# A two-layer graph network on one core: layer 0's edge bias moves from TensorE's bias products to VectorE's additions on the gathered rows

## The reference, cut to what matters

```python
e = edge_attr @ W_edge + b_edge
msg = relu(x[src] + e)
agg = segment_sum(msg, dst, num_segments=x.shape[0])
h = (1.0 + eps) * x + agg
h = relu(h @ W1 + b1) @ W2 + b2      # then batch norm, relu, residual, layer norm
```

## Time and profile before

| | us |
|---|---|
| median of 3 runs | 5301.25 (5294.39 to 5304.22) |
| the profiled execution's own time | 5306.98 |
| its span, first to last instruction | 5305.1 |
| layer 0's edge loop in it | from about 30 to about 2535 |
| layer 1's edge loop in it | from about 2617 to the end |

### The profile page before, as it was taken

One profiled execution on the slowest core, in us unless ns is written; L12 is line 12 of the kernel. 1 busy time (PEld: TensorE's weight loads), 2 busy tenths in 40 slices (PEclk: granted clock), 3 DMA queues, 4 the chain that ended last, 5 costly groups with the idle time before them and its releaser, 6 DMA issues.

```text
span 5305.1 us, 63952 instructions
## 1 busy us (share of the span) xinstructions
PE 3940.2 (74%) x19180; PEld 2743.8 (52%) x19281; DVE 2240.2 (42%) x4481; ACT 718.8 (14%) x1302; POOL 3028.8 (57%) x3229
## 2 busy tenths in 40 slices
PE   6777777778877777777677777776776777777776
PEld 4555555556655555555544444444444444444444
DVE  4333333233332332323544445544555455555555
ACT  2121111112221221112400000000000001001001
POOL 6666656566655555555455555555655555555553
PEclk9888888888888888888877877887877887877777
DMA  4444444344443443433544444444443444443432
GB/s 147 130 132 132 129 126 130 119 131 133 125 129 118 131 128 115 123 115 101 143 122 117 121 120 123 125 120 119 125 119 116 120 124 125 120 123 111 118 114 81
DMA packets 321270, 650.08 MB, mean 123 GB/s; under 512 B 149823, under 2 KB 170537, under 8 KB 321225
## 3 DMA queue, kind: packets, MB, share of 16 engines
q0 software_dynamic: 150272, 413.00, 27.0%
q1 hardware_dynamic: 164681, 230.37, 13.9%
q10 hardware_dynamic: 6272, 6.19, 0.4%
HBM read 636.22 MB, written 13.08 MB: 122 GB/s over the span
## 4 chain that ended last, share of the span: by engine, by line
PE 39%; another core or an unknown queue 24%; issue 18%; DVEq 9%; DVE 8%; ACT 1%; DMA 0%; ACTq 0%; SPq 0%; POOLq 0%
PE psum L685 14%; PE psum L998 7%; PE psum L687 7%; PE psum L1009 5%; DVEq L1152 3%; DVE rows L1136 2%; PE psum L995 1%; DVEq L821 1%; DVE hot_t L854 1%; DVE rows L933 1%; DVEq L863 1%; PE psum L1037 1%; DVEq L1147 1%; DVEq L859 1%
## 5 line engine op out<-in xcount | busy, mean ns | idle before, releaser
L407 POOL DMA_INDIRECT rows<-z_tab,idx x1568 | 1500.3, 957 | 1150.0 <-issue 452.7
L407 POOL DMA_INDIRECT rows<-in_x,idx x1568 | 1491.4, 951 | 1012.4 <-issue 454.2
L685 PE MATMUL psum<-onehot,rows 128*128 128x128 f32 x6272 | 1345.2, 340 | 379.6 <-issue 374.8
L685 PEld LDWEIGHTS psum<-onehot,rows 128*128 128x128 f32 x6272 | 992.9, 223 | 792.1 <-issue 787.5
L1136 DVE TENSOR_TENSOR rows<-rows,psum 128x1024 f32<-128x1024 f32 x392 | 475.6, 1221 | 1706.1 <-remote 1065.9
L998 PE MATMUL psum<-weights,edge_room 128*128 128x256 f32 x3136 | 899.5, 411 | 120.5 <-issue 84.7
L1009 PE MATMUL psum<-rows,onehot 128*128 128x256 f32 x3136 | 860.1, 411 | 130.6 <-issue 126.0
L687 PE MATMUL psum<-onehot,rows 128*4 128x128 f32 x3136 | 687.2, 303 | 129.3 <-issue 128.5
L998 PEld LDWEIGHTS psum<-weights,edge_room 128*128 128x128 f32 x3136 | 658.0, 210 | 233.5 <-issue 78.8
L1009 PEld LDWEIGHTS psum<-rows,onehot 128*128 128x128 f32 x3136 | 627.9, 207 | 263.4 <-issue 184.5
L1082 ACT ACTIVATE rows<-rows 128x1024 f32<-128x1024 f32 x392 | 414.3, 1057 | 1981.3 <-DVE rows L1136 1565.6
(11 more groups left out here) (152 smaller groups left out, 1461.5 us busy)
## 6 DMA issues: line engine op xcount, KB each, us to landing
dst_t<-in_dst_jp SPq DMA_DIRECT2D x197, 512.0 KB
edge_room<-in_edge_t SPq DMA_DIRECT2D x196, 512.0 KB
rows<-in_x,idx POOLq DMA_INDIRECT x1568
rows<-z_tab,idx POOLq DMA_INDIRECT x1568
z_tab<-edge_room SPq DMA_DIRECT2D x14, 455.0 KB, 6.5
idx<-in_src_idx SPq DMA_DIRECT2D x392, 4.0 KB
dst_t<-in_x_t SPq DMA_DIRECT2D x14, 448.0 KB
rows<-in_x_t SPq DMA_DIRECT2D x14, 448.0 KB, 5.1
```

Source lines behind the costliest of these rows:

```text
L407: nc.gpsimd.indirect_dma_start(rows[0:count, u, j, 0:width], None, table, bass.IndirectOffsetOnAxis(ap=idx[0:count, u, j:j + 1], axis=0)). ...
L685: pe.matmul(banks[first + k][:, 0:WIN], rows[:, u, j, k * P:(k + 1) * P], hot, start=(j == 0), stop=(j == J - 1))
```

## The change

The bias products and everything that prepares them go. DVE adds `b_edge`, broadcast over four edges, to each half of the gathered rows, in two instructions ahead of the group's first `add_edges`, with a drain behind them. The edge products now start their banks themselves.

```diff
--- before.py
+++ after.py
@@ -156,10 +156,6 @@
         is_before = early[:, 32 * D:32 * D + GROUPS]
         wz_tmp = early[:, 40 * D:44 * D].rearrange("p (m n) -> p m n", n=D)
         att = hot_t[:, :].bitcast(F32).rearrange("p (a n) -> p a n", a=2)
-        bias_rest = early[:, 36 * D:38 * D].rearrange("p (a n) -> p a n", a=2)
-        bias_part = early[:, 38 * D:39 * D].bitcast(BF16).rearrange("p (a n) -> p a n", a=2)
-        bias_rhs = onehot[:, 2, 0:2, :].rearrange("p j n -> p (j n)").bitcast(BF16)
-        ones_bf = onehot[:, 2, 2, 0:P // 2].bitcast(BF16)
         plan_f = early[0:1, 24 * D:24 * D + 3 * GROUPS].rearrange("p (a n) -> p a n", a=3)
 
 
@@ -260,7 +256,7 @@
                 self.dst_in = [s(f"dst_in_{u}_") for u in range(2)] if n else []
 
         layer0, layer1 = Layer(0), Layer(1)
-        half_done, added, bias_ready = sem("half_done"), sem("added"), sem("bias_ready")
+        half_done, added = sem("half_done"), sem("added")
         a_sum = sem("a_sum")
 
         def two(name):
@@ -990,13 +986,9 @@
                     pe.wait_ge(layer0.edge_in[u], 16 * i + 16)
                 if not (first_round(i) and g == 0):
                     pe.wait_ge(added, 2 * g + b - 1)
-                for q in range(2):
-                    bank = banks[2 * b + q]
-                    pe.matmul(bank[:, 0:2 * D], ones_bf[:, :], bias_rhs[:, :], start=True, stop=False)
-                    for h in range(2):
-                        j = 4 * b + 2 * q + h
-                        last = pe.matmul(bank[:, h * D:(h + 1) * D], edge_in[:, u, j * P:(j + 1) * P], w_edge[:, :],
-                                         start=False, stop=(h == 1))
+                for j in range(4 * b, 4 * b + 4):
+                    last = pe.matmul(banks[j // 2][:, (j % 2) * D:(j % 2 + 1) * D], edge_in[:, u, j * P:(j + 1) * P],
+                                     w_edge[:, :], start=True, stop=True)
                 return last
 
             def sum_half(u, g, b, early):
@@ -1060,7 +1052,6 @@
                 pe.wait_ge(a_act2, c + 1)
                 second_product(c)
 
-            pe.wait_ge(bias_ready, 1)
             pe.wait_ge(const_in, 16 * WEIGHT_LOADS)
             c0 = rounds(pe, body, finish_nodes)
             u = lambda g: g % RING
@@ -1130,6 +1121,10 @@
             def step():
                 dve.drain()
 
+            def add_bias(u, b):
+                half = rows[:, u, 4 * b:4 * b + 4, 0:D]
+                dve.tensor_tensor(half, half, b_edge[:, :].unsqueeze(1).to_broadcast([P, 4, D]), ALU.add)
+
             def add_edges(i, u, g, b):
                 dve.wait_ge(half_done, 2 * g + b + 1)
                 half = rows[:, u, 4 * b:4 * b + 4, 0:D]
@@ -1153,6 +1148,9 @@
 
             def body(i, u, g):
                 dve.wait_ge(layer0.rows_in[u], 16 * J * (i + 1))
+                add_bias(u, 0)
+                add_bias(u, 1)
+                dve.drain()
                 add_edges(i, u, g, 0)
                 make_onehot(u, g)
                 if not (first_round(i) and g < 3):
@@ -1516,25 +1514,6 @@
             dve.drain().then_inc(wz_cols, 1)
 
             dve.wait_ge(edge_w_in, 48)
-            dve.memset(ones_bf[:, :], 1.0)
-            dve.tensor_copy(bias_part[:, 0, :], b_edge[:, :])
-            step()
-            dve.tensor_tensor(bias_rest[:, 0, :], b_edge[:, :], bias_part[:, 0, :], ALU.subtract)
-            step()
-            dve.tensor_copy(bias_part[:, 1, :], bias_rest[:, 0, :])
-            step()
-            dve.tensor_tensor(bias_rest[:, 1, :], bias_rest[:, 0, :], bias_part[:, 1, :], ALU.subtract)
-            dve.tensor_scalar(bias_rhs[:, 0:D], bias_part[:, 0, :], ident[:, 0:1], None, ALU.mult)
-            step()
-            dve.tensor_copy(bias_rhs[:, D:2 * D], bias_rest[:, 1, :])
-            dve.scalar_tensor_tensor(bias_rhs[:, 0:D], bias_part[:, 1, :], ident[:, 1:2], bias_rhs[:, 0:D],
-                                     ALU.mult, ALU.add)
-            step()
-            dve.scalar_tensor_tensor(bias_rhs[:, 0:D], bias_rhs[:, D:2 * D], ident[:, 2:3], bias_rhs[:, 0:D],
-                                     ALU.mult, ALU.add)
-            step()
-            dve.tensor_copy(bias_rhs[:, D:2 * D], bias_rhs[:, 0:D])
-            dve.drain().then_inc(bias_ready, 1)
 
             dve.wait_ge(dst_in, 48)
             dve.tensor_copy(first_f[:, :], firsts[:, 0, :])
```

## The result

The change makes the kernel faster. It was measured twice more, on two chips: 0.9929 (0.9899 to 0.9959) and 0.9899 (0.9876 to 0.9922). The prediction had 5382 us, a loss of 1.5%.

The account below looks back on a forecast made before the run. Layer 0 was taken as bound by POOL: runs of gathers, each with a tail of 2 to 4 us. -13 - 2 + 96 = +81 us on the profiled 5306.98 gave 5388, or 5382 against the runs shown; range 5290 to 5480.

Parts of the forecast that it names:

- Gathers held: POOL's gathers in layer 0, held when starting under DVE's SBUF additions: 0.5 us a group, +96 us, bounds 0 and +419.
- Absorbed: Rival, POOL's waits in layer 0: the holds come off the 2.9 us of waits, 5305 down to 5290; chance 0.12.
- Bias products off PE: Restarts after layer 0's 14 chunk ends: fewer products before the edge product, -13 us, bounds 0 and -24; start -2.
- DVE: Two additions and drain per layer 0 group: 2.6 us, 510 us in all, hidden in DVE's idle time, so zero.
- DVE late: Rival, behind long waits: additions delay a pair's second half by 2.5 us and break runs, +98 us, 5480; chance 0.10.
- PE's gain alone: Rival, POOL's runs in layer 0: additions don't reach POOL's beat, -15 to -24 us, 5286; chance 0.15.
- Preparation and start: Before the loop: 3.5 us of small DVE instructions go, worth nothing, or -3.5 us without the opening run's cover.
- Layer 1: Layer 1's stretch: its code is untouched, so it keeps its length.
- the prediction's +81 us: Whole kernel: sum of -13, -2 and +96, on the profiled 5306.98, so 5388; 5382 against the runs shown.

Follow-up runs that it names:

- the kernel with both: Kernel before with DVE's two bias additions and drain put in, PE's bias products kept, so bias is added twice: 0.9993, again 0.9979.
- the pause: Memset and drain on GpSimd after each group's fourth gather: kernel after without additions 1.1392 (doubled 1.1711), kernel before 1.1412, on a 4100 us chip.
- bias in PSUM: Kernel after with the additions' second operand read from PSUM instead of SBUF, same count and length: 0.9983, again 0.9971.
- no bias: Kernel after without DVE's two bias additions and drain, layer 0's edge bias left out altogether: 1.0023, again 1.0057.
- products twice: Kernel before with each of TensorE's bias products issued twice, no additions on VectorE: 1.0003.
- before with odd: Kernel before, POOL's odd groups waiting for one more half of TensorE's, forcing the order of runs: 1.0035 on a 4089 us chip, 1.0159 on a 5283 us chip.
- half the products: Kernel before with DVE's two additions and drain put in, TensorE's bias products left in each group's first half only: 1.0182 on a 4100 us chip.
- the four with odd or even groups: One more half awaited by odd groups in kernel before 1.0035, after 1.0171, after with PSUM bias 1.0084; by even groups in before 1.0129.

## Why the prediction was wrong

**Gathers held, +96 us: the size was right, the account was not.** 0.070 us x 1536 = 108 us of holds are in the profile, 0.56 us a group where the prediction took 0.5; the mean of 1020 ns and one gather in eight over 1 us are as foretold. What failed is the sentence before it, that the tail "isn't a backlog that a slower POOL would work off meanwhile", drawn from two tails of 4.1 and 3.5 us after runs of 16 and 32. In steady runs the tail shrank by what the run grew. The two tails also did not cover the short runs: in the profile before, the tail behind a run of 8 is 2.6 us in the median and behind a run of 16 4.1, so it does grow with the run there. And the kernel with both, which has the holds and TensorE's full load, costs nothing (0.9993, 0.9979). The rival "Absorbed" had this mechanism and a chance of 0.12, and priced it at 5305 to 5290 because it left out the next point.

**Bias products off PE, -13 us at the chunk ends: wrong by its place.** The prediction shortened each restart by the products' own time. The span from L1164 to the restart is 15.5 us before and 15.6 after; over all profiles on chips of the first kind it is 14.9 to 16.5, so a saving of 0.9 us there can be neither seen nor excluded. What changed is how much of the gathering lies under it, 47 us in this pair of profiles. The prediction looked at one chunk end; five of the 13 waits were over 16 us and eight were 6.0 to 11.2, and that spread was the thing to explain. Neither part of the change does it alone. That most of the gain sits at the chunk ends is shown by the table. That the order of the runs sets their waits is shown by the eight and five waits of the kernel before and by the 13 of 13 of the forced order, but that order, by hand, did not bring the gain. That holds make the start of three groups, and light groups make it regular, is what the last column counts (0, 5 and 6, 12); why they do, and by what path a hold lets a third group in, is open, since the pause meant to test it cost 3 us and landed on a chip without tails.

**DVE.** The two additions took 2.35 us together and cost nothing visible in steady groups, as foretold; its idle time before L1131 fell by 581 us against the 510 us of the estimate. "DVE late" (98 us) did not come; on the fast chip a loss of 22 us at the chunk ends came with the additions, a place that the rival did not name.

**PE's gain alone** named 5286. The time came out on its side, but not for its reason: without holds there was no gain at all (1.0023, 1.0057).

**Preparation and start.** -7.3 us in this pair, but the start of the same kernel after was 57.2 and 58.4 us in its other profiles: no effect that can be told from chance. **Layer 1** was to keep its length. It took 2666, 2670 and 2667 us in the three profiles of the kernel after and 2648 before. Of the other kernels only the one with the bias in PSUM has this too (2666 and 2668); no bias, both, products twice and before with odd took 2646 to 2656. So the longer layer 1, some 15 us lost, goes with additions and no bias products in layer 0; why is open.

**What was not in the prediction at all** is that its subject differs between chips. On two of the chips POOL has no tails in layer 0; there such kernels cost 74.6 us (half the products) and 55 us (by the quotient above). That this is near the prediction's +81 is in part luck: the holds were 47 to 49 us in place of 96, and the chunk ends lost where it had them gain.

## What to carry to other kernels

When an engine runs in bursts, the time that a burst loses inside and the wait behind it are one quantity until an experiment separates them: price a hold against the tail before adding it. Where a few long waits stand among many short ones, list them all; their spread says more than their mean, and here it held most of the gain. Change one part at a time and also both: this gain was in neither part. And before a 1% change is kept, measure it on more than one chip, since here it lost where POOL had no tails, as far as a quotient of two variants can tell.

## What the runs showed of the hardware

- The same kernel before takes 5282 to 5303 us on some chips and 4089 to 4100 us on others (medians). Gathers (946 to 950 ns) and PSUM additions (1.22 us) last the same on both. The difference in layer 0 is that TensorE's updates are seen late. By the modelled ends of its products, VectorE started over 8 us behind in 106 of 392 halves before and in 52 after on the first kind of chip, in none of 392 in either of two profiles from the second. Waits for rows are in that; a group's second half has none, and there VectorE started more than 1 us behind both that end and its own last instruction in 74 of 196 cases before (up to 13.0 us) and 77 after, and in none in the five profiles of half the products and the four with odd or even groups on the second kind (at most 0.2 us). The cause is open.
- A VectorE `tensor_tensor` with both inputs in SBUF holds a gather that begins under it until some 0.13 us before its own end; the gather then takes its usual 0.95 us (1.80 and 1.88 us in all). In the kernel after a held gather ends 0.82 us behind the addition in the median. A `tensor_tensor` with an input in PSUM does not hold it (mean 949 ns).
- GpSimd's drain between gathers: with a memset of 0.54 us it opened 3.12 us between two gathers; a second memset and drain added (2629.1 - 2509.9) / 192 = 0.62 us, little more than the memset. So the first drain seems to have waited some 2.3 us for something that the gather before it had left (an estimate from these two figures).
